# Twenty fields selected and twelve gathered in every unit, and each gather issued when the rows of the one in front of it have landed

## Chip, cores and metric

The kernel runs on one core of a Trainium2 chip. The metric is the device time in microseconds of one execution; of several executions the median counts.

## What is computed

A batch of 2048 samples has 32 categorical fields. Each field has its own table of rows of 64 floats (1000, 1250, 12500 or 125000 rows). For every sample the 32 rows are looked up, all pairs of them are multiplied (a Gram matrix of 32 by 32, of which the 496 entries above the diagonal count), 16 dense values are put behind, and a tower of three layers follows:

```python
e = jnp.stack([tbl_0[ids[:, 0]], ..., tbl_31[ids[:, 31]]], axis=1)
gram = jnp.einsum('bnd,bmd->bnm', e, e)
z = gram[:, rows, cols]                      # rows < cols
h = jnp.concatenate([z, dense_ctx], axis=1)
h = jnp.maximum(h @ W_top1 + b_top1, 0.0)    # 512 -> 512
h = jnp.maximum(h @ W_top2 + b_top2, 0.0)    # 512 -> 256
y = h @ W_top3                               # 256 -> 1
```

## The kernel before

The batch is cut into four units of 512 samples, and each unit into two rounds (halves of 256 samples). A field's rows reach the tensor `vecs` in one of two ways.

**Gathered fields.** GpSimd issues an indirect DMA (L296) that brings 128 rows of one field from its table in HBM into `rows`. One field, one round and one half of the round's samples make one gather; 16 fields make 64 gathers in a unit. TensorE turns them (`turn`, L513: a transposition into `gat_ps`, four fields together), and ScalarE copies them to `vecs` (L337). A turn waits until the semaphore `rows_in[r][x]` counts all its gathers, 16 counts for each. Between two gathers GpSimd writes zeros into a spare tile that nobody reads (L303): a fill of 1024 columns in unit 0 and of 512 in the others. A gather never waits for another. It waits only for the turn of the unit before that emptied its part of `rows` (L292).

**Selected fields.** Small tables (1000 or 1250 rows) are held on chip as three bf16 parts, `tabs`, packed so that a row number is a partition and a chunk: 8 chunks for 1000 rows, 10 for 1250. For each chunk VectorE compares the broadcast sample indices `ids_wide` with the chunk's row numbers and writes a one-hot matrix (L453). TensorE multiplies table parts and one-hots into `sel_ps` (`select`, L498): three matmuls for a chunk and field. Fields go in pairs; one-hots come in pieces (half of a field's chunks) through a ring of four. ScalarE copies the result to `vecs` (L329). The tables are loaded and split once, in unit 0, by `high` and `middle` on ScalarE (L317, L322) and two subtractions on VectorE (L436, L441). SP loads `ids_wide` for the next unit pair by pair, 256 KB each (L197), as soon as the one-hots of that pair are done.

In units 0 and 3 sixteen fields (eight pairs) are selected and sixteen gathered (four turns). In units 1 and 2 the last pair is gathered too: seven pairs, five turns, the last of them with two fields:

```python
SHIFTED = (1, 2)
ROWS_OF = GATHERED + SELECTED[-2:]
PAIRS = [ALL_PAIRS - (u in SHIFTED) for u in range(UNITS)]
TURNS = [ALL_TURNS - (u not in SHIFTED) for u in range(UNITS)]
```

**The rest of a unit.** When all 32 fields of a round are in `vecs`, TensorE forms the products (`gram`, L528: 512 small matmuls a round, in four calls). ScalarE and VectorE copy them to `work` (L346, L460), SP writes them to HBM (L206 to L209) and reads them back as diagonals (L224 to L228) for the tower (L542, L551, L560). The tower of a unit runs between the products of the next. All orders are written out by hand. On TensorE a unit is: the rest of its selection with the turns of round 0 among the last pairs; products of round 0 with the first layer of the unit before between them; the turns of round 1, with two selections of the next unit among them; products of round 1 with the second and third layer of the unit before between them. After unit 3 come the tower passes of its two rounds.

The names used below: `gather(u, r, x)` and `turn(u, r, x)` are for unit u, round r and group x of four fields.

## Time and profile before

| | us |
|---|---|
| median of 3 runs | 574.52 (572.3 to 587.05) |
| the profiled execution, its own time | 577.56 |
| its span, first to last instruction | 575.8 |
| GpSimd busy | 465.0 |
| TensorE busy | 403.8 |
| VectorE busy | 292.7 |
| ScalarE busy | 141.8 |

Busy time is the union of an engine's instructions. In the rows below an arrow names what a row waited for last, and a time in front of it the idle time that ended so. Positions are microseconds from the span's start. "PEclk" is the clock granted to TensorE as a share of 2.4 GHz. A DMA instruction's own row is the time for issuing it, not the time in which data move; these are seen in the DMA share, the mean busy share of the core's 16 DMA engines.

### The profile page before, as it was taken

What the parts mean: (1) busy time and instruction counts of PE and PEld (TensorE: products, weight loads), DVE (VectorE), ACT (ScalarE), POOL (GpSimd) and SP (SyncE); (2) the same over time, 40 slices, a digit from 0 to 9 for tenths busy, and PEclk for the clock granted to TensorE, in tenths of its full rate; (3) what the DMA queues carried; (4) which work ended last, traced back from release to release, by engine and by line L of the source; (5) the groups of instructions that cost most, each with busy time, mean ns of one, the idle gap of its engine ahead of it and who ended that gap; (6) DMA issues with size and microseconds to landing.
All of it is one profiled execution on the core that took longest, in us unless ns stands there. A gap on an engine that the chain in (4) does not pass through costs nothing.

```text
span 575.8 us, 13498 instructions
## 1 busy us (share of the span) xinstructions
PE 403.8 (70%) x5956; PEld 217.7 (38%) x5956; DVE 292.7 (51%) x513; ACT 141.8 (25%) x232; POOL 465.0 (81%) x552
## 2 busy tenths in 40 slices
PE   0556554756874678787975687868966788799877
PEld 0222222323543334334432344334432344445655
DVE  4999999999180299300810499100900599100000
ACT  5002233422200334310201434111110434212212
POOL 7999999999998899989998999889988999950000
PEclk9977778787695699888986799887996799989989
DMA  8414311110111475110111584101011651003340
GB/s 271 140 51 141 98 33 32 30 35 15 21 21 23 73 166 150 29 23 20 22 21 23 101 190 124 23 21 21 21 23 23 132 119 19 19 16 64 72 83 1
DMA packets 39060, 36.11 MB, mean 63 GB/s; under 512 B 14869, under 2 KB 27991, under 8 KB 38874
## 3 DMA queue, kind: packets, MB, share of 16 engines
q1 hardware_dynamic: 29866, 25.14, 18.0%
q0 software_dynamic: 8704, 8.93, 7.6%
q8 instruction: 47, 0.77, 0.5%
q10 hardware_dynamic: 432, 1.18, 0.5%
q14 instruction: 11, 0.09, 0.0%
HBM read 27.15 MB, written 8.07 MB: 61 GB/s over the span
## 4 chain that ended last, share of the span: by engine, by line
PE 42%; DVE 39%; issue 11%; ACT 4%; DMA 2%; SPq 2%; ACTq 0%; DVEq 0%
DVE onehot L453 35%; PE gram_ps L528 14%; PE tower_ps L542 11%; PE sel_ps L498 9%; PE tower_ps L551 5%; ACT vecs L329 2%; PE tower_ps L560 2%; DVE work L436 2%; DVE tabs L441 2%; PE gat_ps L513 2%; DMA work<-in_packed_dram 1%; ACT work L346 1%; SPq L207 1%; DMA products<-work 1%; SPq L209 1%
## 5 line engine op out<-in xcount | busy, mean ns | idle before, releaser
L453 DVE TENSOR_SCALAR onehot<-ids_wide,row_ids 128x512 bf16<-128x512 f16 x488 | 269.4, 627 | 113.2 <-PE sel_ps L498 113.2
L296 POOL DMA_INDIRECT rows<-in_tbl_dram,gat_ids x272 | 287.0, 1055 | 46.3 <-issue 44.3
L498 PE MATMUL sel_ps<-onehot,tabs 128*64 128x512 bf16 x1464 | 200.4, 433 | 98.1 <-DVE onehot L453 79.5
L303 POOL MEMSET spare<- 128x512 f32 (+1 forms) x272 | 177.9, 654 | 0.1
L498 PEld LDWEIGHTS sel_ps<-onehot,tabs 128*64 128x64 bf16 x1464 | 95.9, 123 | 196.8 <-issue 95.2
L528 PE MATMUL gram_ps<-vecs 64*32 64x32 f32 x4096 | 71.2, 214 | 61.4 <-issue 48.8
L329 ACT COPY vecs<-sel_ps 64x256 f32<-64x256 f32 x120 | 71.9, 599 | 123.1 <-PE sel_ps L498 70.2
L528 PEld LDWEIGHTS gram_ps<-vecs 64*32 64x32 f32 x4096 | 54.6, 115 | 93.7 <-issue 80.5
L542 PE MATMUL tower_ps<-work,w_sb 128*128 128x512 f32 (+1 forms) x160 | 73.8, 622 | 2.8 <-DMA work<-products 2.8
L460 DVE COPY work<-gram_ps 128x512 f32<-128x512 f32 x8 | 5.2, 687 | 127.9 <-PE gram_ps L528 127.9
L542 PEld LDWEIGHTS tower_ps<-work,w_sb 128*128 128x128 f32 x160 | 35.7, 230 | 31.4 <-issue 25.3
L352 ACT ACTIVATE h<-tower_ps,b_sb 128x512 f32<-128x512 f32 (+1 forms) x20 | 12.0, 602 | 81.2 <-PE tower_ps L542 81.2
L551 PE MATMUL tower_ps<-h,w_sb 128*128 128x512 f32 (+1 forms) x80 | 31.0, 537 | 1.1 <-ACT h L352 1.1
L337 ACT COPY vecs<-gat_ps 128x512 f32<-128x512 f32 (+1 forms) x36 | 19.5, 570 | 34.8 <-PE gat_ps L513 29.5
L346 ACT COPY work<-gram_ps 128x512 f32<-128x512 f32 x24 | 13.0, 588 | 59.3 <-PE gram_ps L528 59.3
L322 ACT CAST tabs<-work 128x1024 bf16<-128x1024 f32 (+1 forms) x8 | 8.6, 1072 | 70.0 <-DVE work L436 70.0
L513 PE MATMUL gat_ps<-ident,rows 128*128 128x128 f32 x136 | 21.7, 293 | 4.9 <-ACT vecs L337 4.9
L513 PEld LDWEIGHTS gat_ps<-ident,rows 128*128 128x128 f32 x136 | 15.1, 145 | 14.4 <-issue 8.6
L551 PEld LDWEIGHTS tower_ps<-h,w_sb 128*128 128x128 f32 x80 | 15.1, 197 | 12.5 <-issue 9.7
L359 ACT ACTIVATE h<-tower_ps,b_sb 128x512 f32<-128x512 f32 (+1 forms) x10 | 5.5, 598 | 36.3 <-PE tower_ps L551 36.3
L560 PE MATMUL tower_ps<-h,w_sb 128*1 128x512 f32 (+1 forms) x20 | 11.1, 689 | 1.9 <-ACT h L359 1.9
L436 DVE TENSOR_TENSOR work<-work,tabs 128x1024 f32<-128x1024 f32 (+1 forms) x8 | 10.0, 1248 | 4.2 <-ACT tabs L317 4.2
(13 smaller groups left out, 25.1 us busy)
## 6 DMA issues: line engine op xcount, KB each, us to landing
ids_wide<-ids_scratch SPq DMA_DIRECT2D x30, 256.0 KB
rows<-in_tbl_dram,gat_ids POOLq DMA_INDIRECT x272
products<-work SPq DMA_DIRECT2D x12, 248.0 KB
products<-work SPq DMA_DIRECT2D x24, 120.0 KB
work<-in_packed_dram SPq DMA_DIRECT2D x5, 512.0 KB, 4.4
work<-products SPq DMA_DIRECT2D x9, 256.0 KB
work<-in_packed_dram ACTq DMA_DIRECT2D x2, 512.0 KB, 6.1
w_sb<-in_w_dram SPq DMA_DIRECT2D x1, 1024.0 KB
```

The costliest lines, as they stand in the source:

```text
L296: nc.gpsimd.indirect_dma_start(out=rows[:, r, k, h, :], out_offset=None, in_=tables[ROWS_OF[k]], in_offset=bass.IndirectOffsetOnAxis(ap=ga ...
L303: nc.gpsimd.memset(spare[:, 0:SPACING[u]], 0.0).then_inc(spaced, 1)
L329: last = nc.scalar.copy(vecs[DIM * h:DIM * h + DIM, :, N_GAT + 2 * g + at], sel_ps[DIM * at:DIM * at + DIM, sel_no(u, g) % 2, HALF * h:HAL ...
L337: nc.scalar.copy(vecs[:, P * r:P * r + P, at], gat_ps[:, n % 2, 0:P * fields].rearrange("p (f j) -> p j f", f=fields))\
L436: nc.vector.tensor_tensor(piece, piece, tabs[:, c0:c0 + k, 0, :], ALU.subtract).then_inc(rest_ready, 1)
L453: last = nc.vector.tensor_scalar(onehot[:, n % RING, c - c0, :], ids_wide[:, k, :], row_ids[chunks[k]][:, c:c + 1], None, ALU.is_equal)
L498: last[at] = nc.tensor.matmul(sel_ps[DIM * at:DIM * at + DIM, n % 2, :], tabs[:, first_chunk[k] + c, part, :], onehot[:, piece_no(u, g, ha ...
L513: last = nc.tensor.transpose(gat_ps[:, n % 2, P * at:P * at + P], rows[:, r, k, :, :].rearrange("p h d -> p (h d)"), ident[:])
L528: last = nc.tensor.matmul(gram_ps[32 * s:32 * s + 32, h, i, :], v, v, start=True, stop=True, skip_group_check=True)
L542: last = nc.tensor.matmul(tower_ps[:, j % 2, 0:width], w1_sb[:, c, P * j:P * j + P], z[:, c, x0:x0 + width], start=(c == 0), stop=(c == Q ...
L551: last = nc.tensor.matmul(tower_ps[:, o, 0:width], w2_sb[:, j, P * o:P * o + P], h1[:, j, 0:width], start=(j == 0), stop=(j == J1 - 1), sk ...
L560: last = nc.tensor.matmul(tower_ps[0:1, 0, 0:width], w3_sb[:, o:o + 1], h2[:, o, 0:width], start=(o == 0), stop=(o == J2 - 1))
```

## The change

Four things change. All units have the same plan: ten pairs selected and three turns gathered, so twelve gathered fields. Six tables of 1250 rows are now among the selected ones: of the sixteen selected before, two had 1250 rows. The fills are gone. And each gather is followed by a wait for its own sixteen counts, so that GpSimd issues the next when all of its rows have landed. The last pairs of a unit (from the eighth on) are where the turns of round 0 stand.

```diff
-SELECTED = [7, 8, 9, 11, 12, 15, 17, 18, 20, 22, 24, 25, 27, 28, 30, 31]
+SELECTED = [7, 8, 9, 11, 12, 15, 17, 18, 20, 22, 24, 25, 27, 28, 16, 21, 23, 29, 30, 31]
 GATHERED = [f for f in range(FIELDS) if f not in SELECTED]
...
+GROUPS = [range(k, min(k + 4, N_GAT)) for k in range(0, N_GAT, 4)]
+N_PAIRS, N_TURNS = N_SEL // 2, len(GROUPS)
...
-SPACING = [1024, 512, 512, 512]
...
             def gather(u, r, x):
-                for v in [v for v in range(u) if x < TURNS[v]][-1:]:
-                    pool.wait_ge(gat_full, gat_no(v, r, x) + 1)
-                for k in range(N_ROWS)[turn_slots(x)]:
+                if u > 0:
+                    pool.wait_ge(gat_full, gat_no(u - 1, r, x) + 1)
+                for k in GROUPS[x]:
                     for h in range(2):
-                        at = ((u * ROUNDS + r) * 2 + h) * N_ROWS + k
+                        at = ((u * ROUNDS + r) * 2 + h) * N_GAT + k
                         nc.gpsimd.indirect_dma_start(
-                            out=rows[:, r, k, h, :], out_offset=None, in_=tables[ROWS_OF[k]],
+                            out=rows[:, r, k, h, :], out_offset=None, in_=tables[GATHERED[k]],
                             in_offset=bass.IndirectOffsetOnAxis(ap=gat_ids[:, at:at + 1], axis=0))\
                           .then_inc(rows_in[r][x], 16)
-                        spaced_no = next(count)
-                        if spaced_no > 0:
-                            pool.wait_ge(spaced, spaced_no)
-                        nc.gpsimd.memset(spare[:, 0:SPACING[u]], 0.0).then_inc(spaced, 1)
+
+                        so_far = 2 * len(GROUPS[x]) * u + 2 * (k - GROUPS[x].start) + h + 1
+                        pool.wait_ge(rows_in[r][x], 16 * so_far)
...
             for u in range(UNITS):
-                for g in range(2, PAIRS[u]):
+                for g in range(2, N_PAIRS):
                     select(u, g)
-                    if g >= 4:
-                        turn(u, 0, g - 4)
-                for x in range(PAIRS[u] - 4, TURNS[u]):
-                    turn(u, 0, x)
+                    if g >= N_PAIRS - N_TURNS:
+                        turn(u, 0, g - N_PAIRS + N_TURNS)
...
-                for x in range(3, TURNS[u]):
+                for x in range(3, N_TURNS):
                     turn(u, 1, x)
```

The other engines' loops run over `N_PAIRS` and `N_TURNS` in the same way: `load_wide` on SP has ten loads a unit, and the table loads and subtractions of unit 0 are ten.

GpSimd's instructions at the start of the gathers, before (`ident` is the unit matrix of the turns, `spare` the tile of the fills):

```order
L285 AFFINE_SELECT ident<-ident 128x128 [waits ident_zero]
L296 DMA rows<-in_tbl_dram,gat_ids 128x64 [waits gat_ids_in0]
L303 MEMSET spare 128x1024
L296 DMA rows<-in_tbl_dram,gat_ids 128x64
L303 MEMSET spare 128x1024 [waits spaced]
L296 DMA rows<-in_tbl_dram,gat_ids 128x64
L303 MEMSET spare 128x1024 [waits spaced]
```

And the same place now, up to the end of unit 0's gathers (an "x8" is eight such instructions one after the other):

```order
L252 AFFINE_SELECT ident<-ident 128x128 [waits ident_zero]
L261 DMA rows<-in_tbl_dram,gat_ids 128x64 [waits gat_ids_in0]
L261 DMA rows<-in_tbl_dram,gat_ids 128x64 [waits rows_in0_0] x8
L261 DMA rows<-in_tbl_dram,gat_ids 128x64 [waits rows_in0_1] x8
L261 DMA rows<-in_tbl_dram,gat_ids 128x64 [waits rows_in0_2] x8
L261 DMA rows<-in_tbl_dram,gat_ids 128x64 [waits rows_in1_0] x8
L261 DMA rows<-in_tbl_dram,gat_ids 128x64 [waits rows_in1_1] x8
L261 DMA rows<-in_tbl_dram,gat_ids 128x64 [waits rows_in1_2] x7
L261 DMA rows<-in_tbl_dram,gat_ids 128x64 [waits gat_full,gat_ids_in1,rows_in1_2]
```

Between the gathers stand no other instructions any more, and every gather but the first waits for the semaphore of the one in front of it.

TensorE's instructions from the products of unit 0, round 0, to the first layer in unit 1, before (`gram_ps` products, `gat_ps` turns, `sel_ps` selection, `tower_ps` tower):

```order
L528 MATMUL gram_ps<-vecs 32x32 x256
L513 MATMUL gat_ps<-ident,rows 128x128 x8
L498 MATMUL sel_ps<-onehot,tabs 64x512 x48
L513 MATMUL gat_ps<-ident,rows 128x128 x4
L498 MATMUL sel_ps<-onehot,tabs 64x512 x48
L513 MATMUL gat_ps<-ident,rows 128x128 x4
L528 MATMUL gram_ps<-vecs 32x32 x256
L498 MATMUL sel_ps<-onehot,tabs 64x512 x144
L513 MATMUL gat_ps<-ident,rows 128x128 x4
L498 MATMUL sel_ps<-onehot,tabs 64x512 x48
```

And now:

```order
L489 MATMUL gram_ps<-vecs 32x32 x256
L474 MATMUL gat_ps<-ident,rows 128x128 x8
L460 MATMUL sel_ps<-onehot,tabs 64x512 x48
L474 MATMUL gat_ps<-ident,rows 128x128 x4
L460 MATMUL sel_ps<-onehot,tabs 64x512 x48
L489 MATMUL gram_ps<-vecs 32x32 x256
L460 MATMUL sel_ps<-onehot,tabs 64x512 x300
L474 MATMUL gat_ps<-ident,rows 128x128 x4
L460 MATMUL sel_ps<-onehot,tabs 64x512 x60
```

The fourth turn of round 1 is gone; the third, turn (u, 1, 2), now is the last before the products. Behind them 300 matmuls of selection stand where 144 stood.

## Rows read from the trace of the kernel before

**Rows 1.** The page: its span, and section 1, busy time of each engine.
```profile
span 575.8 us, 13498 instructions
PE 403.8 (70%) x5956; PEld 217.7 (38%) x5956; DVE 292.7 (51%) x513; ACT 141.8 (25%) x232; POOL 465.0 (81%) x552
```
**Rows 2.** The chain that ended last: by line, then pieces (start us, us, what).
```profile
by line: DVE onehot L453 35.4%; PE gram_ps L528 13.5%; PE tower_ps L542 11.4%; issue 10.9%; PE sel_ps L498 9.0%; PE tower_ps L551 4.6%; ACT vecs L329 2.5%; PE tower_ps L560 1.7%; DVE work L436 1.6%; DVE tabs L441 1.6%; PE gat_ps L513 1.6%; 
...
87.02 6.33 DVE onehot L453 x8
...
206.36 6.90 DVE onehot L453 x16
...
243.84 3.63 PE tower_ps L542 x8
252.02 5.33 PE tower_ps L542 x8
...
272.93 2.75 PE sel_ps L498 x24
...
523.88 1.15 PE gat_ps L513 x8
...
557.63 10.00 PE tower_ps L542 x32
```
**Rows 3.** One line's instructions: gathers and one-hots (duration ns min/median/max, first and last start us).
```profile
L296 POOL DMA_INDIRECT rows<-in_tbl_dram,gat_ids x272: 950/1062/2204, 3.3 to 510.5; - x136
...
L453 DVE TENSOR_SCALAR onehot<-ids_wide,row_ids x488: 332/342/1759, 12.4 to 490.9; 128x512 bf16<-128x512 f16 x163
```
**Rows 4.** Groups by line and form (busy us, mean ns, idle before and releasers).
```profile
L296 POOL DMA_INDIRECT rows<-in_tbl_dram,gat_ids x272 | 287.0, 1055 | 46.3 <-issue 44.3 <-DMA gat_ids<-in_ids_gat_dram 1.8 <-PE gat_ps L513 0.2
L453 DVE TENSOR_SCALAR onehot<-ids_wide,row_ids 128x512 bf16<-128x512 f16 x488 | 269.4, 627 | 113.2 <-PE sel_ps L498 113.2
...
L303 POOL MEMSET spare<- 128x512 f32 x208 | 115.9, 557 | 0.1
...
L303 POOL MEMSET spare<- 128x1024 f32 x64 | 62.0, 969 | 0.0
...
L436 DVE TENSOR_TENSOR work<-work,tabs 128x1280 f32<-128x1280 f32 x1 | 1.5, 1472 | 0.0
```
**Rows 5.** Slices behind one gather (us; engines; then PEclk, DMA share, GB/s).
```profile
488.30:488.50 0.20, 0.20 (x6) 0.13 (x2) 0.20 (x1) 0.20 (x1) 0.20 (x1) 1.00 0.00 0
488.50:488.70 0.20, 0.20 (x6) 0.12 (x3) 0.20 (x2) 0.10 (x1) 0.04 (x1) 1.00 0.25 61
...
488.90:489.10 0.20, 0.20 (x6) 0.12 (x4) 0.20 (x2) 0.00 (x0) 0.20 (x1) 1.00 0.06 10
489.10:489.30 0.20, 0.20 (x6) 0.12 (x4) 0.20 (x2) 0.00 (x0) 0.20 (x1) 1.00 0.00 0
```
**Rows 6.** Timeline of GpSimd (start us, us; in brackets the idle time before).
```profile
3.31 1.19 POOL L296 DMA_INDIRECT rows<-in_tbl_dram,gat_ids  x1 [1.85 <-DMA gat_ids<-in_ids_gat_dram]
...
26.24 1.94 POOL L296 DMA_INDIRECT rows<-in_tbl_dram,gat_ids  x1 [0.17 <-issue]
...
486.90 1.07 POOL L296 DMA_INDIRECT rows<-in_tbl_dram,gat_ids  x1 [0.16 <-issue]
```
**Rows 7.** The page's section 6, DMA issues (KB each, median us to landing): the index load.
```profile
gat_ids<-in_ids_gat_dram SPq DMA_DIRECT2D x1, 36.0 KB, 2.3
```
**Rows 8.** Timeline of SP's queue: the index load, and the seven broadcasts for unit 2.
```profile
0.74 0.40 SPq L237 DMA_DIRECT2D gat_ids<-in_ids_gat_dram  x1
...
213.41 15.31 SPq L197 DMA_DIRECT2D ids_wide<-ids_scratch  x7
```
**Rows 9.** Slices before the last tower pass, columns as in rows 5.
```profile
556.60:556.80 0.20, 0.00 (x0) 0.00 (x0) 0.00 (x0) 0.00 (x0) 0.00 (x0) 0.50 0.18 51
556.80:557.00 0.20, 0.00 (x0) 0.00 (x0) 0.00 (x0) 0.00 (x0) 0.00 (x0) 0.50 0.02 5
```
**Rows 10.** Windows with busy transfer engines, the first and the last of five.
```profile
0.00:20.00 20.00, 1.08 (x6) 0.63 (x8) 11.48 (x14) 7.36 (x7) 16.41 (x23) 1.00 0.78 265
...
446.00:472.00 26.00, 19.93 (x150) 9.68 (x151) 19.38 (x43) 10.35 (x18) 23.60 (x30) 0.84 0.68 137
```

More of the change, by code:

```diff
@@ L44 @@
 MOVES = 3 * Q
-SPACING = [1024, 512, 512, 512]
-PAIRS = [ALL_PAIRS - (u in SHIFTED) for u in range(UNITS)]
-TURNS = [ALL_TURNS - (u not in SHIFTED) for u in range(UNITS)]
-PAIRS_TO = [sum(PAIRS[:u]) for u in range(UNITS + 1)]
-MOST_PAIRS = max(PAIRS)
-TURNS_TO = [ROUNDS * sum(TURNS[:u]) for u in range(UNITS + 1)]
 def sel_no(u, g):
-    return PAIRS_TO[u] + g
+    return N_PAIRS * u + g
 def gat_no(u, r, x):
-    return TURNS_TO[u] + TURNS[u] * r + x
-def units_with_pair(u, g):
-    return sum(g < PAIRS[v] for v in range(u))
-def units_with_turn(u, x):
-    return sum(x < TURNS[v] for v in range(u))
-def turn_slots(x):
-    return slice(4 * x, min(4 * x + 4, N_ROWS))
-def turn_columns(x):
-    return slice(4 * x, 4 * x + 4) if 4 * x < N_GAT else slice(FIELDS - 2, FIELDS)
+    return N_TURNS * (ROUNDS * u + r) + x
 def emptied_no(u, r, b):
@@ L86, in piece_no @@
 def piece_no(u, g, half, at):
-    return 4 * (PAIRS_TO[u] + g) + 2 * half + at
+    return 4 * (N_PAIRS * u + g) + 2 * half + at
 def pair_row(n, m):
@@ L99, in dlrm_tower_kernel @@
     half_most = max(b - a for h in halves for a, b in h)
-    pair_chunks = [(first_chunk[2 * g], chunks[2 * g] + chunks[2 * g + 1]) for g in range(ALL_PAIRS)]
+    pair_chunks = [(first_chunk[2 * g], chunks[2 * g] + chunks[2 * g + 1]) for g in range(N_PAIRS)]
     pair_most = max(k for _, k in pair_chunks)
-    assert all(chunks[2 * g] == chunks[2 * g + 1] for g in range(ALL_PAIRS))
+    assert all(chunks[2 * g] == chunks[2 * g + 1] for g in range(N_PAIRS))
     with ExitStack() as ctx:
@@ L121, in dlrm_tower_kernel @@
         onehot = sb("onehot", [P, RING, half_most, UNIT], BF16)
-        rows = sb("rows", [P, ROUNDS, N_ROWS, 2, DIM], F32)
+        rows = sb("rows", [P, ROUNDS, N_GAT, 2, DIM], F32)
         vecs = sb("vecs", [P, HALF, FIELDS], F32)
@@ L193, in load_wide @@
             def load_wide(u, w):
-                last = [v for v in range(u) if w < PAIRS[v]][-1:]
-                for v in last:
-                    sp.wait_ge(onehot_ready, piece_no(v, w, 1, 1) + 1)
+                if u > 0:
+                    sp.wait_ge(onehot_ready, piece_no(u - 1, w, 1, 1) + 1)
                 sp.dma_start(ids_wide[:, WIDE * w:WIDE * w + WIDE, :],
@@ L234, in store @@
                   .then_inc(y_out[v % 2], 16)
-            first = ROUNDS * 2 * N_ROWS
+            first = ROUNDS * 2 * N_GAT
             sp.dma_start(gat_ids[:, 0:first], ids_gat[:, 0:first]).then_inc(gat_ids_in[0], 16)
@@ L246, in _ @@
                 load_wide(0, w)
-            for g in range(STAGE_SLOTS, MOST_PAIRS):
+            for g in range(STAGE_SLOTS, N_PAIRS):
                 load_stage(g)
@@ L254, in _ @@
             for u in range(LAST):
-                for w in range(PAIRS[u + 1]):
+                for w in range(N_PAIRS):
                     load_wide(u + 1, w)
@@ L308, in _ @@
                 for r in range(ROUNDS):
-                    for x in range(TURNS[u]):
+                    for x in range(N_TURNS):
                         gather(u, r, x)
@@ L386, in _ @@
             for u in range(UNITS):
[L387 removed]
+                for g in range(2, N_PAIRS):
                     selected(u, g)
[L389 removed]
+                    if u == 0 and g + 4 < N_PAIRS:
                         high(g + 4)
                         middle(g + 4)
[L392 to L395 removed]
+                    if g >= N_PAIRS - N_TURNS:
+                        gathered(u, 0, g - N_PAIRS + N_TURNS)
                 if u == 0:
@@ L405, in _ @@
                 gram(u, 0, 1, (0, 1))
-                for x in range(TURNS[u]):
+                for x in range(N_TURNS):
                     gathered(u, 1, x)
@@ L445, in one_hots @@
                 if half == 0:
[L446 removed]
+                    dve.wait_ge(wide_in[g], 16 * (u + 1))
                 for at in range(2):
@@ L659 @@
     out = nc.dram_tensor("out_0_dram", (BATCH, 1), _mybir.dt.float32, kind="ExternalOutput").ap()
-    tables = {f: args[f"tbl_{f}"] for f in ROWS_OF}
+    tables = {f: args[f"tbl_{f}"] for f in GATHERED}
     chunks = [inputs[f"tbl_{f}"].shape[0] // KROWS for f in SELECTED]
```

48 lines of the change are left out of this document (18 added, 30 removed).

## The prediction

> **What bounds the kernel now.** I began with the shares of the span [rows 1]. GpSimd is busy 465.0 of 575.8 us, more than TensorE (403.8) or VectorE (292.7). The next view to read is the chain of work that ended last [rows 2]: 35% of it is the one-hot instructions of VectorE, the rest mostly TensorE, and GpSimd is not in it. So GpSimd is fullest and yet holds nobody up. The source view of the gathers says why [rows 3]: 272 gathers, the last issued at 510.5 us; before them GpSimd waited 44.3 us for "issue" (0.16 us each), 1.8 us for its index load and 0.2 us for TensorE. It runs without a break from 3.3 us, gather and fill in turn, at a pace that the program chose: 1055 ns for a gather, 557 or 969 ns for a fill [rows 4]. The chain takes up the last transposes at 523.88 [rows 2], some 11 us after those rows came in. The pace of the gathers is hidden, but by about 2% of the span only. That is the number to hold on to.
>
> VectorE is slowed by the same fills. Its one-hots last 332 ns at least and 342 in the median, but 627 in the mean and 1759 at most [rows 3, 4]. In unit 0, with the long fills, eight follow each other in 6.33 us (0.79 us each); later, with short fills, sixteen take 6.9 us (0.43 each) [rows 2]. The Trainium skill ("SBUF — State Buffer", on the shared port pair) says that a VectorE instruction in a two-port mode and a GpSimd instruction exclude each other for their whole length. The trace agrees in size: a 1759 ns one-hot is 1417 ns over the median, one long fill of 969 and some 450 of the gather in front of it. So the fills' removal helps VectorE whatever else happens, and the gathers' share of its delays stays.
>
> **The change, part by part.**
>
> Fills. 272 of them go, 177.9 us of GpSimd [rows 4].
>
> Fields. One-hots rise from 488 to 4 × (14×8 + 6×10) = 688, selecting matmuls from 1464 to 2064, gathers fall from 272 to 4 × 2 × 12 × 2 = 192. Without fills I take 0.34 us for a one-hot, so a unit costs VectorE 172 × 0.34 = 58 us. TensorE needs about 2.8 us for the 24 matmuls of half a pair [rows 2], so a unit's 14 halves of 24 and 6 halves of 30 take 14×2.8 + 6×3.4 = 60 us. Unit 0, where the first plan spent 132 × 0.79 = 104 us on one-hots, saves about 37 us net of six more table subtractions of 1.47 us [rows 4]. Units 1 and 2 have three pairs more and two turns fewer: about +12 us each. Unit 3 has 8 pairs after its first two where it had 6, but each at TensorE's pace: about nothing. So TensorE's and VectorE's side, if nothing else held it, would shrink by 37 − 24 = 13 us, and by up to 24 us more where the issue gaps of TensorE in the pair products get fewer. This is the gain that the change could have.
>
> The new wait. Every gather now waits until the rows of the one before it have landed. Queued behind that wait on GpSimd is nothing but the other gathers; the order shows it. TensorE waits for them: turn (u,1,2) needs all 48 gathers of its unit, and behind it in TensorE's stream stand the second half's pair products and the next unit's selection. So GpSimd's time becomes one sum, 192 times the cycle of a gather.
>
> The cycle has three pieces. (1) From the start of a gather to the end of its data. The gather that starts at 486.90 [rows 6] has its traffic in the slices from 488.5 to 489.1, with silence before and after [rows 5]: 2.0 to 2.2 us. (2) From the data's end to the semaphore, and (3) from the semaphore to the next start. The trace never shows GpSimd waiting for gathered rows, so these are bounded by neighbours. At the kernel's start the index load, issued at 0.74, lands 2.3 us later, at 3.04, and GpSimd's first gather starts at 3.31: 0.27 us for (3) [rows 6 to 8]. The last wait of TensorE for a transfer gives (2) and (3) together: the share of the DMA engines is down to 0.02 at 556.8 to 557.0, and the matmul starts at 557.63: 0.65 us or a little more [rows 2, 9]. Lower end: 2.1 + 0.45 = 2.55 us. Upper end: 2.2 + 0.75 = 2.95 us. I take 2.7. Against it stands the 1.7 us of gather, fill and issue on which the old kernel ran (1.06 + 0.56 + 0.16, [rows 4]). Even with no fill the new cycle is a microsecond longer; 192 × 2.7 = 518 us, where 272 gathers took 507.
>
> On this the Trainium skill ("DMA: Bandwidth & Descriptors", on the anatomy of a DMA issued by GpSimd) speaks for the change: about 2.0 us plus bytes over 436 GB/s from issue to completion. By its figures, as an estimate, a gather of 32 KB would take 2.08 us and 192 of them 399 us, and they would be hidden with ease. The trace does not agree: the data alone end after 2.0 to 2.2 us, and the semaphore and the restart come on top.
>
> Busy transfer engines. In five stretches the share of the DMA engines is 0.68 to 0.78: 0 to 20, 48 to 62, 194 to 228, 320 to 350 and 446 to 472, in all 124 us (the first and the last of the five stand in [rows 10]). There a gather's packets stand among those of the broadcasts and the products. Ten more broadcasts of 256 KB (40 for 30) at 15.31/7 = 2.2 us each [rows 8] add 22 us: 146 us. Before, such a delay cost nothing, since GpSimd didn't look; now each is on the path. A gather in such a stretch may be held by nothing or by a whole broadcast (2.2 us), and two to three things are queued there, so I take 1.5 us: 146/4.2 = 35 gathers × 1.5 = 52 us. Bounds: 20 and 66 us. In unit 0 a table subtraction can hold a gather (1.94 us instead of 1.07 [rows 6]): 20 subtractions × 0.35 = 7 us.
>
> The tail. From the last transposes at 523.88 to the span's end are 52 us [rows 1, 2]. It stays, since every step hangs on the last rows: the second layer, the last products, their way through memory, the last tower passes. After a wait of some 20 us TensorE would begin it at the lower of its two levels, as at 556.6 to 557.0 after a short pause [rows 9] (granted clock 0.50 is 1.2 GHz, 1.00 is 2.4). Eight tower matmuls take 5.3 us where the clock is low for 3.6 at the full one [rows 2]; two such groups come first, so I add 3 us.
>
> **The sum.** 3.3 (start) + 518 + 52 + 7 + 52 + 3 = 635 us of span. The profiled execution was 577.6 for a span of 575.8, so 637; the median of the runs shown is 3 us under the profiled time, so 634 us. GpSimd ends its last gather near 581 us instead of 512, and drags the rest along. TensorE's gain of 13 us or more disappears in its wait for turn (u,1,2).
>
> **Rivals.**
> (a) The gathers remain hidden, and the faster VectorE shows. That needs a cycle of at most 2.45 us and little delay in busy stretches: 192 × 2.45 = 470, so the last rows land at 475 to 490. The end is then TensorE's: 574.5 − 13 = 561 down to 537, say 548 us. For it: 465 us of GpSimd work shrink to 203 us of gathers, and VectorE is 35% of the chain. Against it: the pieces of the cycle measure more. It decides from a cycle of 2.5 us down. Chance 0.06.
> (b) The new wait just cancels the gain. Cycle 2.55 us, busy stretches cost 20 us: 3.3 + 490 + 20 + 52 = 565, time 564 to 586. For it: one gather in flight at a time may slip through the queues better than two. Chance 0.10.
> (c) Worse than forecast. Cycle 2.95 us, 66 us in busy stretches, 14 us from the subtractions and a tail of 55: 705 us; in part, above 668. For it: the 0.65 us between data and matmul at the end. Against it: that one moved more data to HBM and back. Chance 0.08.
> Forecast 0.76.
>
> **Range.** Low end: cycle 2.6 (499) + 3.3 + 30 + 52 + 1.8 = 586. High end: 2.8 (538) + 3.3 + 66 + 7 + 55 = 669. A measurement of this kernel can tell about 2% from no change (563 to 586). Slower by more: (c), the forecast: 0.84. Within: (b) 0.10. Faster by more: (a) 0.06.
>
> **What would show it.** GpSimd's gathers start 2.6 to 2.8 us apart in quiet stretches, and about 4 in those with a DMA share near 0.7; the last one starts near 578 us of the span. The releaser of GpSimd's waits is the DMA of rows; TensorE's transposes show long waits of 10 us and more once a unit; the one-hots' mean is near their old median of 342 ns, and VectorE and TensorE are busy less than 60% of the span. The granted clock falls in each wait. Wrong would be the sum if starts lie under 2.5 us apart, if the last transposes don't wait, or if the time from them to the end isn't 50 to 56 us.

## The result, and the profile after

The changed kernel takes 675.27 us (673.14 to 677.21, four executions) beside 573.41 us (571.43 to 587.05) of the kernel before: a ratio of 1.178, 95% interval 1.174 to 1.183. Some executions of a kernel run longer at a lower granted clock; medians and ranges here are of all executions, ratios leave those out, and "like with like" below does too. The forecast was 634 us with a range of 586 to 669. The direction and the mechanism came true, and the time lies 6 us above the range.

The page of the changed kernel, its span, busy times, granted clock and DMA share, the chain that ended last, and two of its groups (columns as in [rows 1, 4]):

```profile
span 671.3 us, 14540 instructions
PE 420.5 (63%) x6516; PEld 234.6 (35%) x6516; DVE 222.4 (33%) x717; ACT 166.6 (25%) x264; POOL 204.0 (30%) x200
...
PEclk9999975557759987957698996957688999755899
DMA  7453100000037410000007710000007300320040
...
DMA 77%; issue 13%; PE 5%; POOL 3%; SPq 1%; DVE 0%; ACT 0%; POOLq 0%
...
L261 POOL DMA_INDIRECT rows<-in_tbl_dram,gat_ids x192 | 203.1, 1058 | 411.2 <-DMA rows<-in_tbl_dram,gat_ids 405.2
L415 DVE TENSOR_SCALAR onehot<-ids_wide,row_ids 128x512 bf16<-128x512 f16 x688 | 193.7, 354 | 279.4 <-PE sel_ps L460 278.0
...
L474 PE MATMUL gat_ps<-ident,rows 128*128 128x128 f32 x96 | 20.9, 356 | 187.4 <-DMA rows<-in_tbl_dram,gat_ids 187.4
```

GpSimd has fallen from the fullest engine (81% in [rows 1]) to one of the emptiest (30%), and is now the bound. Busy shares hide this; the chain shows it. Before, it consisted of one-hots and matmuls [rows 2]; now 77% of it is DMA, nearly all of it the landing of gathered rows. The idle time before the gathers, 46.3 us in [rows 4], is 411.2, of which 405.2 ended with rows that landed. TensorE's turns wait 187.4 us for the same rows. Each long stretch of 5 to 7 in PEclk is such a wait.

The waits of the changed kernel: engine and line, what for, us in all, times, longest:

```profile
POOL rows L261 <- DMA rows<-in_tbl_dram,gat_ids: 405.2, 190, 5.4
DVE onehot L415 <- PE sel_ps L460: 278.0, 55, 65.7
...
PE gat_ps L474 <- DMA rows<-in_tbl_dram,gat_ids: 187.4, 14, 21.3
```

VectorE's 278 us are the longest of all in this list after the gathers, and mean nothing: its one-hots are early, and wait for TensorE to free the ring.

The source view of the gathers and of the one-hots (as [rows 3]), and how long a gather's rows took to land:

```profile
L261 POOL DMA_INDIRECT rows<-in_tbl_dram,gat_ids x192: 943/946/4463, 3.4 to 614.8; - x192
...
DMA to landing us min/median/max: 2.3/2.5/8.3
```

A quiet place, GpSimd's timeline (as [rows 6]) and the slices behind the gather at 126.91 (as [rows 5]):

```profile
124.17 0.94 POOL L261 DMA_INDIRECT rows<-in_tbl_dram,gat_ids  x1 [1.72 <-DMA rows<-in_tbl_dram,gat_ids]
126.91 0.95 POOL L261 DMA_INDIRECT rows<-in_tbl_dram,gat_ids  x1 [1.80 <-DMA rows<-in_tbl_dram,gat_ids]
129.60 0.95 POOL L261 DMA_INDIRECT rows<-in_tbl_dram,gat_ids  x1 [1.74 <-DMA rows<-in_tbl_dram,gat_ids]
```
```profile
128.30:128.50 0.20, 0.00 (x0) 0.00 (x0) 0.00 (x0) 0.00 (x0) 0.00 (x0) 0.50 0.00 0
128.50:128.70 0.20, 0.00 (x0) 0.00 (x0) 0.00 (x0) 0.00 (x0) 0.00 (x0) 0.50 0.74 124
128.70:128.90 0.20, 0.00 (x0) 0.00 (x0) 0.00 (x0) 0.00 (x0) 0.00 (x0) 0.50 0.27 41
128.90:129.10 0.20, 0.00 (x0) 0.00 (x0) 0.00 (x0) 0.00 (x0) 0.00 (x0) 0.50 0.02 0
129.10:129.30 0.20, 0.00 (x0) 0.00 (x0) 0.00 (x0) 0.00 (x0) 0.00 (x0) 0.50 0.00 0
```

Starts are 2.74 and 2.69 us apart. Nothing moves for the first 1.6 us; the data are through in some 0.4 us; then 0.6 to 0.7 us pass until the next start. The transfer itself is the small part of a cycle.

The same in windows of 24 gathers each, the eight halves of the four units (columns: length; busy time and count of TensorE, its weight loads, VectorE, ScalarE, GpSimd; granted clock; DMA share; GB/s):

```profile
3.40:104.50 101.10, 61.27 (x525) 31.41 (x526) 76.46 (x209) 47.11 (x63) 38.82 (x25) 0.93 0.39 131
104.50:172.80 68.30, 18.39 (x573) 11.95 (x574) 4.65 (x16) 3.91 (x7) 22.67 (x25) 0.55 0.07 12
172.80:258.70 85.90, 64.02 (x993) 36.61 (x993) 44.80 (x158) 27.09 (x45) 25.43 (x25) 0.84 0.33 77
258.70:326.10 67.40, 31.32 (x605) 16.57 (x605) 4.40 (x16) 6.56 (x11) 22.65 (x25) 0.73 0.07 13
326.10:409.50 83.40, 71.69 (x1013) 39.13 (x1014) 44.92 (x158) 28.90 (x48) 24.48 (x24) 0.93 0.35 79
409.50:475.70 66.20, 32.90 (x605) 17.13 (x606) 4.64 (x16) 6.56 (x11) 22.76 (x24) 0.71 0.07 13
475.70:550.10 74.40, 69.75 (x978) 37.97 (x980) 41.00 (x142) 26.54 (x44) 23.56 (x25) 0.92 0.28 53
550.10:617.50 67.40, 26.65 (x593) 14.58 (x590) 0.00 (x0) 8.94 (x15) 22.64 (x24) 0.72 0.19 36
```

This table is the whole result. At 2.7 us a cycle, 24 gathers take 64.8 us. The second half of every unit comes close (66.2 to 68.3: together 10 us more than four times 64.8). The first halves, in which one-hots, broadcasts and products run, take 101.1, 85.9, 83.4 and 74.4: 86 us more than 2.7 a cycle. In the second halves TensorE is busy for 18 to 33 us of 67, and its granted clock is 0.55 to 0.73.

### The profile page after: what moved, and what is told of

The parts are those of the page before. It is cut to its first block, busy times and chain, and to the rows that moved or that the text cites. A ratio compares the mean times of both kernels' runs of the same rounds, so it can differ in the third digit from the quotient of the medians.

```text
span 671.3 us, 14540 instructions
## 1 busy us (share of the span) xinstructions
PE 420.5 (63%) x6516; PEld 234.6 (35%) x6516; DVE 222.4 (33%) x717; ACT 166.6 (25%) x264; POOL 204.0 (30%) x200
## 2 busy tenths in 40 slices
DMA packets 38232, 37.48 MB, mean 56 GB/s; under 512 B 13781, under 2 KB 26903, under 8 KB 38042
## 4 chain that ended last, share of the span: by engine, by line
DMA 77%; issue 13%; PE 5%; POOL 3%; SPq 1%; DVE 0%; ACT 0%; POOLq 0%
DMA rows<-in_tbl_dram,gat_ids 76%; POOL rows L261 3%; PE tower_ps L512 2%; PE tower_ps L503 1%; PE gram_ps L489 1%; PE tower_ps L521 1%; SPq L176 1%; DMA products<-work 0%; DMA gat_ids<-in_ids_gat_dram 0%; DMA work<-products 0%; SPq L174 0%; SPq L173 0%; DVE work L422 0%; SPq L191 0%; PE gat_ps L474 0%
## 5 line engine op out<-in xcount | busy, mean ns | idle before, releaser
L261 POOL DMA_INDIRECT rows<-in_tbl_dram,gat_ids x192 | 203.1, 1058 | 411.2 <-DMA rows<-in_tbl_dram,gat_ids 405.2
L415 DVE TENSOR_SCALAR onehot<-ids_wide,row_ids 128x512 bf16<-128x512 f16 x688 | 193.7, 354 | 279.4 <-PE sel_ps L460 278.0
L460 PE MATMUL sel_ps<-onehot,tabs 128*64 128x512 bf16 x2064 | 247.7, 401 | 34.2 <-ACT vecs L293 17.9
L460 PEld LDWEIGHTS sel_ps<-onehot,tabs 128*64 128x64 bf16 x2064 | 128.7, 116 | 148.3 <-issue 48.4
L474 PE MATMUL gat_ps<-ident,rows 128*128 128x128 f32 x96 | 20.9, 356 | 187.4 <-DMA rows<-in_tbl_dram,gat_ids 187.4
L293 ACT COPY vecs<-sel_ps 64x256 f32<-64x256 f32 x160 | 96.7, 605 | 105.4 <-PE sel_ps L460 93.4
L301 ACT COPY vecs<-gat_ps 128x512 f32<-128x512 f32 x24 | 14.1, 588 | 206.6 <-PE gat_ps L474 206.4
L489 PE MATMUL gram_ps<-vecs 64*32 64x32 f32 x4096 | 50.7, 210 | 22.0 <-issue 14.1
L489 PEld LDWEIGHTS gram_ps<-vecs 64*32 64x32 f32 x4096 | 43.5, 112 | 45.1 <-issue 37.3
L286 ACT CAST tabs<-work 128x1024 bf16<-128x1024 f32 (+1 forms) x10 | 11.1, 1109 | 26.3 <-DVE work L398 26.3
L403 DVE TENSOR_TENSOR tabs<-work,tabs 128x1024 bf16<-128x1024 f32 (+1 forms) x10 | 13.0, 1295 | 1.1 <-ACT tabs L286 1.1
L281 ACT CAST tabs<-work 128x1024 bf16<-128x1024 f32 (+1 forms) x10 | 11.1, 1108 | 3.5 <-DMA work<-in_packed_dram 3.4
```

The source lines that it names most:

```text
L261: nc.gpsimd.indirect_dma_start(out=rows[:, r, k, h, :], out_offset=None, in_=tables[GATHERED[k]], in_offset=bass.IndirectOffsetOnAxis(ap=g ...
L293: last = nc.scalar.copy(vecs[DIM * h:DIM * h + DIM, :, N_GAT + 2 * g + at], sel_ps[DIM * at:DIM * at + DIM, sel_no(u, g) % 2, HALF * h:HAL ...
L301: nc.scalar.copy(vecs[:, P * r:P * r + P, at:at + fields], gat_ps[:, n % 2, 0:P * fields].rearrange("p (f j) -> p j f", f=fields))\
L403: nc.vector.tensor_tensor(tabs[:, c0:c0 + k, 2, :], stage[g % STAGE_SLOTS][:, 0:k, :], tabs[:, c0:c0 + k, 1, :], ALU.subtract).then_inc(ta ...
L415: last = nc.vector.tensor_scalar(onehot[:, n % RING, c - c0, :], ids_wide[:, k, :], row_ids[chunks[k]][:, c:c + 1], None, ALU.is_equal)
L460: last[at] = nc.tensor.matmul(sel_ps[DIM * at:DIM * at + DIM, n % 2, :], tabs[:, first_chunk[k] + c, part, :], onehot[:, piece_no(u, g, ha ...
```

## The experiments

The runs were made on four chips, here A to D, which give the kernel before 557.6 (A), 567 (B), 557.1 (C) and 557.9 us (D). Each ratio is to the kernel before on the same chip. It matters below. On which chip the first measurement ran isn't on record; the kernel before took 573.41 us there, more than on any of the four.

**Which part of the change costs the time.** First the changed kernel without its wait, nothing else (chip A):

```diff
-                        so_far = 2 * len(GROUPS[x]) * u + 2 * (k - GROUPS[x].start) + h + 1
-                        pool.wait_ge(rows_in[r][x], 16 * so_far)
```

> The changed kernel without the wait behind each gather (still no fills). Theory (the serial cycle of 192 gathers is the whole slowdown): GpSimd issues gathers every 1.1 to 1.2 us, is held only by the turns of the unit before, the transposes no longer wait 187 us, and the time is that of TensorE's side, 530 to 565 us. Rival (the field split, 2064 selecting matmuls for 1464, is what costs): 620 us or more, with TensorE waiting for one-hots or ScalarE instead.

Measured: 461.84 us, ratio 0.829 (0.824 to 0.834). The page's line of the gathers, and the products:

```profile
L261 POOL DMA_INDIRECT rows<-in_tbl_dram,gat_ids x192 | 186.3, 970 | 152.0 <-PE gat_ps L471 93.4 <-issue 56.7 <-DMA gat_ids<-in_ids_gat_dram 1.9
...
L486 PE MATMUL gram_ps<-vecs 64*32 64x32 f32 x4096 | 53.0, 209 | 18.8 <-issue 8.8 <-ACT work L307 4.9 <-ACT vecs L298 2.7
```

The gathers wait for TensorE again, which empties their tensor, and not for their rows. The two lines of code cost some 210 us: the changed kernel takes 672 to 677 us on every chip that ran it. The version is faster by far more than I had expected of it; why it is, and that it isn't on every chip, comes below.

Then the new split of fields with the fills as they were, in place of the wait (chip A):

```diff
-                        so_far = 2 * len(GROUPS[x]) * u + 2 * (k - GROUPS[x].start) + h + 1
-                        pool.wait_ge(rows_in[r][x], 16 * so_far)
+                        spaced_no = next(count)
+                        if spaced_no > 0:
+                            pool.wait_ge(spaced, spaced_no)
+                        nc.gpsimd.memset(spare[:, 0:SPACING[u]], 0.0).then_inc(spaced, 1)
```

> The new field split with the old fills (1024 columns in unit 0, 512 after) instead of the wait. Theory: gathers go out every 1.75 to 2.2 us, 192 of them end by 400 us and hold nobody; one-hots are back at 0.43 us in the later units and 0.79 in unit 0, so about 172 x 0.79 = 136 us for unit 0's selection and 172 x 0.43 = 74 for each other unit: 590 to 630 us, slower than without fills by 40 us or more. Rival (fills cost VectorE nothing on the path): same as the run without them, within 1%.

Measured: 529.69 us, ratio 0.951 (0.947 to 0.956). So I was wrong on the sign: twenty selected fields are worth 28 us even with the fills, although the one-hots last 515 ns in the mean (in the profile of an execution of 541.43 us).

And the other half alone, the old split with the wait in place of the fills (chip A, one execution):

```diff
-                        spaced_no = next(count)
-                        if spaced_no > 0:
-                            pool.wait_ge(spaced, spaced_no)
-                        nc.gpsimd.memset(spare[:, 0:SPACING[u]], 0.0).then_inc(spaced, 1)
+                        landed[r, x] = landed.get((r, x), 0) + 1
+                        pool.wait_ge(rows_in[r][x], 16 * landed[r, x])
```

> The kernel before with the new wait in place of the fills, field split as before (272 gathers). Theory: GpSimd's chain is 3.3 + 272 x 2.70 = 738 us and 90 to 100 us of delays in stretches with busy transfer engines, plus 54 of tail: about 885 us. Rival (the split costs, not the wait): below 675 us.

Measured: 881.98 us, as expected. Its waits:

```profile
POOL rows L296 <- DMA rows<-in_tbl_dram,gat_ids: 536.0, 268, 6.4
...
PE gat_ps L511 <- DMA rows<-in_tbl_dram,gat_ids: 442.2, 31, 22.8
```

The rule "so many gathers by one cycle, plus delays, plus the tail" carries over to 272 gathers. The two parts of the change are nothing alike: the split gains, the wait loses, and the fewer gathers of the new split only soften the wait.

**Is it the wait as such, or one gather at a time?** A semaphore for each half h, and each gather waits for the one before the last, so that two are in flight (chip A):

```diff
-        rows_in = [[sem(f"rows_in{r}_{x}") for x in range(N_TURNS)] for r in range(ROUNDS)]
+        rows_in = [[[sem(f"rows_in{r}_{x}_{h}") for h in range(2)] for x in range(N_TURNS)] for r in range(ROUNDS)]
...
+                        if landing[h]:
+                            pool.wait_ge(*landing[h])
...
-                          .then_inc(rows_in[r][x], 16)
+                          .then_inc(rows_in[r][x][h], 16)
...
+                        landing[h] = (rows_in[r][x][h], 16 * (len(GROUPS[x]) * u + k - GROUPS[x].start + 1))
```

> The changed kernel with two gathers in flight: each half h has a semaphore of its own and a gather waits for the rows of the one before the last. Theory: two gathers per cycle of 2.7 to 2.9 us, 192 in about 270 us plus delays, so GpSimd is never last outside unit 0 and the time is that of the run without waits, within 2%. Rival (GpSimd needs the whole landing time for itself, or the port is the limit): cycle of a gather stays above 2 us, time above 600 us.

Measured: 471.31 us, ratio 0.841 (0.831 to 0.850), 2% over the kernel without the wait. GpSimd still waits 141.7 us for rows, and it costs 9 us. What hurt was that a whole landing stood between any two gathers.

**What lengthens the cycle in the first halves.** The changed kernel once more on chip B:

> The changed kernel itself, as the yardstick for the other runs of this call: 660 to 680 us, GpSimd's gathers 2.7 us apart in quiet stretches.

Measured: 677.43 us, ratio 1.196 (1.185 to 1.206).

Theory one: a gather is held as long as VectorE's one-hots follow each other without a gap. In units 1 to 3 each one-hot gets a second one in front, which nobody reads (chip B):

```diff
+                        if u > 0:
+                            no = next(extras)
+                            if no >= 4:
+                                dve.wait_ge(extra_done, no - 3)
+                            nc.vector.tensor_scalar(extra[:, no % 4, :], ids_wide[:, k, :],
+                                                    row_ids[chunks[k]][:, c:c + 1], None, ALU.is_equal)\
+                              .then_inc(extra_done, 1)
```

> The changed kernel with a second, unused one-hot ahead of each one-hot in units 1 to 3, so that VectorE has fewer gaps there. Theory (a gather that starts while VectorE's one-hots follow without a gap is kept from finishing until the next gap, as in unit 0): the gathers' mean in the selection stretches of the later units rises from 0.95 to 1.06 us to 1.5 us or more, with single ones of 3 us and over, and the time by 20 to 60 us over the changed kernel. Rival (unit 0's long gathers come from the table loads and subtractions there): gathers stay at 0.94 to 1.1 us in the later units, and the time within 1% of the changed kernel.

Measured: 847.02 us (825.68 to 849.09): 170 us over the unchanged kernel, and like with like still 148, where I expected 20 to 60. GpSimd's gathers are busy for 392.4 us, 2044 ns each in the mean, beside 195.8 us and 1020 ns in the unchanged kernel on the same chip, so the gathers that last longer account for the loss and more. The gathers by source, and a piece of GpSimd's timeline:

```profile
L263 POOL DMA_INDIRECT rows<-in_tbl_dram,gat_ids x192: 942/942/54732, 3.3 to 790.5; - x192
```
```profile
635.11 5.57 POOL L263 DMA_INDIRECT rows<-in_tbl_dram,gat_ids  x1 [2.71 <-DMA rows<-in_tbl_dram,gat_ids]
643.32 54.73 POOL L263 DMA_INDIRECT rows<-in_tbl_dram,gat_ids  x1 [2.64 <-DMA rows<-in_tbl_dram,gat_ids]
699.74 0.94 POOL L263 DMA_INDIRECT rows<-in_tbl_dram,gat_ids  x1 [1.69 <-DMA rows<-in_tbl_dram,gat_ids]
```

One gather lasts 54.73 us where the median is 0.94. Over that stretch VectorE shows:

```profile
643.40:698.00 54.60, 32.38 (x268) 16.54 (x268) 53.84 (x206) 14.46 (x25) 54.60 (x1) 0.94 0.09 20
```

It is busy 53.84 of 54.60 us with 206 instructions, and the DMA share is 0.09, so it isn't busy transfer engines that hold the gather. It fits the mechanism for which the prediction cited the Trainium skill ("SBUF — State Buffer", "Who interferes with whom", on the shared port pair): VectorE in a two-port mode and GpSimd exclude each other. The trace doesn't show the ports or the mode of a one-hot; it shows that the two engines don't take turns here: VectorE, back to back, kept the gather out for 54 us. In the changed kernel gathers are held for a shorter time. GpSimd's gathers in unit 0, while one-hots and table subtractions follow each other:

```profile
24.12 4.46 POOL L261 DMA_INDIRECT rows<-in_tbl_dram,gat_ids  x1 [1.84 <-DMA rows<-in_tbl_dram,gat_ids]
30.31 3.34 POOL L261 DMA_INDIRECT rows<-in_tbl_dram,gat_ids  x1 [1.73 <-DMA rows<-in_tbl_dram,gat_ids]
...
40.49 3.17 POOL L261 DMA_INDIRECT rows<-in_tbl_dram,gat_ids  x1 [3.45 <-DMA rows<-in_tbl_dram,gat_ids]
```
```profile
23.05 2.19 DVE L415 TENSOR_SCALAR onehot<-ids_wide,row_ids 128x512 bf16<-128x512 f16 x8
25.15 1.22 DVE L398 TENSOR_TENSOR work<-work,tabs 128x1024 f32<-128x1024 f32 x1
26.28 2.19 DVE L415 TENSOR_SCALAR onehot<-ids_wide,row_ids 128x512 bf16<-128x512 f16 x8
```

All gathers together are 21.7 us over 192 × 0.945 (busy 203.1), 16 of it in the first half of unit 0 (38.82 − 22.7 in the window table). There each of the ten gathers that last over 1.3 us overlaps a table subtraction as well as one-hots, so that what each of the two holds isn't separated; in units 1 to 3, where one-hots are alone, it is some 6 us, with single gathers of 2.83 and 1.93 us. And gathers were held before the change, too: 272 of them were busy for 287.0 us [rows 4], 30 us over 272 × 0.945, but nobody waited for them.

Theory two: the broadcasts hold the gathers. In units 1 to 3 they bring 32 of the 512 samples' indices, and what the one-hots of those units select is left wrong (chip B):

```diff
-                sp.dma_start(ids_wide[:, WIDE * w:WIDE * w + WIDE, :],
-                             ids_scratch[u, WIDE * w:WIDE * w + WIDE, :].partition_broadcast(P))\
+                n = UNIT if u == 0 else UNIT // 16
+                sp.dma_start(ids_wide[:, WIDE * w:WIDE * w + WIDE, 0:n],
+                             ids_scratch[u, WIDE * w:WIDE * w + WIDE, 0:n].partition_broadcast(P))\
```

> The changed kernel with the index broadcasts of units 1 to 3 cut to 32 of 512 samples (the other samples keep the indices of unit 0, so their selected rows are those of other samples). Theory (half of the delays in busy stretches is the broadcasts'): GpSimd's chain gets shorter by 30 to 45 us, time 630 to 645. Rival (the products on their way through memory, or something else, delay the gathers): less than 12 us shorter, 660 or more.

Measured: 669.96 us, ratio 1.179 (1.170 to 1.188), 7 us under the unchanged one on the same chip. Its first halves of units 1 to 3:

```profile
170.60:252.60 82.00, 64.78 (x993) 37.57 (x994) 45.27 (x158) 27.10 (x45) 24.20 (x25) 0.85 0.28 51
320.90:403.50 82.60, 70.55 (x1013) 38.96 (x1014) 45.44 (x158) 28.97 (x48) 26.18 (x24) 0.93 0.28 50
469.20:546.30 77.10, 70.04 (x978) 38.00 (x980) 41.24 (x142) 26.52 (x44) 23.50 (x25) 0.91 0.27 51
```

They take 241.7 us where those of the unchanged kernel on chip B take 247.8 (85.1, 84.7, 78.0). So the bytes of the broadcasts cost 6 to 7 us. What the broadcasts as such cost isn't settled: all thirty still run, with 16 KB in place of 256, land after 4.8 us in the median where 5.7 was usual, and the run has more packets than before (42072 for 38232).

Theory three, what is left: the transfers of products. Each of the twelve writes of units 0 to 2 is made twice, the second time into a tensor that nobody reads (chip C):

```diff
                 for s in range(Q):
-                    rows_out(u, s, slice(0, P), slice(P * s, P * s + P))
+                    rows_out(u, s, slice(0, P), slice(P * s, P * s + P), products)
+                    rows_out(u, s, slice(0, P), slice(P * s, P * s + P), copies)
```

> The changed kernel; in units 0 to 2 each of the twelve writes of products is made twice, the second time into a tensor that nobody reads. Theory: a gather waits its turn among the transfers of products, about 1.6 us each, in some 20 us per unit, of which the writes are more than half. Twice the writes are some 10 us more of such a stretch per unit, with periods of 4 to 5 us where 2.7 stood: 8 to 14 us a unit, so 700 to 717 us. Rival: the excess comes from instruction loads and TensorE's or VectorE's work in that phase, not from the transfers: 675 to 685 us.

Measured: 690.32 us (682.20 to 697.45), beside 671.87 (664.71 to 687.43) of the changed kernel, moved by 1056 bytes, on the same chip. Like with like it is 684.5 beside 667.1 us (two executions and three): 17 us, where I expected 28 to 45. The same three windows:

```profile
178.00:263.80 85.80, 63.77 (x993) 37.17 (x994) 44.98 (x158) 27.06 (x45) 24.70 (x25) 0.86 0.45 100
...
331.00:416.00 85.00, 69.83 (x1013) 38.63 (x1014) 45.83 (x158) 28.95 (x48) 23.40 (x25) 0.94 0.46 101
...
481.00:563.30 82.30, 73.08 (x1013) 39.58 (x1014) 40.92 (x142) 28.87 (x48) 24.80 (x24) 0.93 0.38 73
```

The DMA share rises from 0.34, 0.34 and 0.26 in the profile of the moved kernel to 0.45, 0.46 and 0.38. The windows alone don't show the cost: they take 253.1 us, and those of the moved kernel, profiled in its execution of 687.43 us, 252.6 (86.9, 85.7, 80.0). The packet records show it. In units 1 to 3, 12 gathers of the moved kernel land late while SP issues writes of products or just behind them, by 21 us in all; with the writes doubled it is 23 gathers and 33 us. (On the other two chips the unchanged kernel has 14 gathers and 17 us, and 13 and 18.) So transfers of products do hold gathers, and twice the writes hold about twice as many, each for no longer: a gather started at 205.17, amid the doubled writes, has its successor 3.33 us later, and one at 200.56, amid the single ones of the changed kernel, 3.33 us later too. That is 12 to 16 us more for the three units, where I expected 24 to 42.

**Why 462 us, and not everywhere.** On chip B three kernels with bare gathers, no fill and no wait. First the old split:

```diff
-                        spaced_no = next(count)
-                        if spaced_no > 0:
-                            pool.wait_ge(spaced, spaced_no)
-                        nc.gpsimd.memset(spare[:, 0:SPACING[u]], 0.0).then_inc(spaced, 1)
```

> The kernel before with neither fills nor waits, 272 gathers one behind the other. Theory (the fills alone held the old kernel, and the new split is worth little by itself): gathers 1.25 us apart, 470 to 490 us. Rival (the gain over the old kernel that was seen without waits comes from the new split): above 520 us.

Measured: 666.20 us, ratio 1.171 (1.163 to 1.179): 100 us slower than with the fills, where the new split without its wait had been 17% faster on chip A. Two of its lines:

```profile
L494 PE MATMUL sel_ps<-onehot,tabs 128*64 128x512 bf16 x1464 | 215.8, 419 | 139.9 <-issue 92.3 <-DVE onehot L449 35.2 <-ACT vecs L325 10.3
...
L524 PE MATMUL gram_ps<-vecs 64*32 64x32 f32 x4096 | 64.3, 215 | 94.8 <-issue 82.4 <-ACT vecs L333 6.8 <-ACT work L342 4.7
```

TensorE stands idle with "issue", that is, for no reason that the profile knows. I looked for it in the split, by sixteen selected fields in all units (old kernel, bare) and by eighteen (new kernel, bare):

```diff
-SHIFTED = (1, 2)
+SHIFTED = ()
```

> Sixteen fields selected and sixteen gathered in all units, no fills, no waits (256 gathers). Theory S with the number of gathers as the cause: between 560 and 660 us, with stalls beside the gathers in proportion to 256 against 272. If only the fifth turn did it: below 520 us. Theory P says nothing about it.

```diff
-SELECTED = [7, 8, 9, 11, 12, 15, 17, 18, 20, 22, 24, 25, 27, 28, 16, 21, 23, 29, 30, 31]
+SELECTED = [7, 8, 9, 11, 12, 15, 17, 18, 20, 22, 24, 25, 27, 28, 16, 21, 30, 31]
```

> Eighteen fields selected and fourteen gathered in all units (fourth turn with two fields), no fills, no waits: 224 gathers. Without stalls in TensorE's issue it has 20 one-hots and 60 selecting matmuls a unit less than the version with twenty and twelve, some 7 us a unit less for TensorE and one turn more: 440 to 455 us, faster than 462. With stalls as in the old split: 520 us or more.

Measured: 645.15 and 621.36 us, ratios 1.136 (1.128 to 1.144) and 1.096 (1.089 to 1.104). And in the placement of the tensors in memory, by an unused tensor of 264 words in front of all others, once with the old split and once with the new one:

```diff
+        pad = sb("pad", [P, 264], F32)
         ident = sb("ident", [P, P], F32)
```

> The old split with neither fills nor waits, and one unused tensor of 264 words a partition allocated first, so that all tensors on chip lie 1056 bytes further up; nothing else differs. Theory P (TensorE's issue stalls of 0.7 us beside gathers depend on where the tensors lie): the time moves by more than 5% from 666 us. Theory S (they belong to the old split itself, more gathers and other streams): 650 to 680 us, the stalls as before.

> The new split with neither fills nor waits, and the same unused tensor in front. Theory P: the stalls come in, and the time rises from 462 us by more than 5%. Theory S: 455 to 472 us, no stalls.

Measured: 665.36 us, the same as unmoved on this chip (666.20), and 622.41 us, ratio 1.096 (1.090 to 1.103). The second looked like a proof: the kernel of 461.84 us, moved by 1056 bytes, takes 160 us more. It was none, since the two had run on different chips. Smaller moves on chip C, by 256 and by 8 words in place of 264, didn't bring the stalls back:

> The kernel without the wait, all tensors 1024 bytes higher (before: 1056 bytes made it 622 us where it took 462). If the 32 bytes beyond a multiple of 1024 (or of 64) decide, this one is back at 460 to 475 us; if the move by a kilobyte decides, it is near 620 us.

> The kernel without the wait, all tensors 32 bytes higher. If the alignment to 64 bytes decides, near 620 us; if only moves of about a kilobyte matter, 460 to 475 us. Should both this and the move by 1024 bytes stay near 462, neither part alone explains the 622.

Measured: 464.24 and 465.81 us, ratios 0.836 both. So the two kernels of the false proof ran side by side on chip D:

> The kernel without the wait once more, beside the one moved by 1056 bytes on the same chip. Until now the two were timed on different chips. If placement makes the difference: 460 to 470 us. If the chip makes it, this one is slow here when the moved one is, near 620 us, or both are near 465.

> The kernel without the wait and all tensors 1056 bytes higher, once more, beside the unmoved one on the same chip. If placement makes the difference: 615 to 625 us beside 460 to 470 for the unmoved one. If the chip or the run makes it, the two are within 2% of each other.

Measured: 465.15 us and 466.52 us. Placement does nothing, neither on chip D nor, with the old split, on chip B. The same kernel takes 622 us on chip B and 467 us on chip D. TensorE's timeline on chip B, then on chip D:

```profile
43.30 0.58 PE L458 MATMUL sel_ps<-onehot,tabs 128*64 128x512 bf16 x1 [2.90 <-issue]
45.41 0.59 PE L458 MATMUL sel_ps<-onehot,tabs 128*64 128x512 bf16 x1 [1.52 <-issue]
48.20 0.58 PE L458 MATMUL sel_ps<-onehot,tabs 128*64 128x512 bf16 x1 [2.21 <-issue]
```
```profile
38.61 5.56 PE L458 MATMUL sel_ps<-onehot,tabs 128*64 128x512 bf16 x48 [1.93 <-ACT vecs L291]
46.09 5.57 PE L458 MATMUL sel_ps<-onehot,tabs 128*64 128x512 bf16 x48 [1.92 <-ACT vecs L291]
```

On B there is one matmul in 2.1 to 2.8 us; on D 48 of the same instructions take 5.56 us. In both GpSimd issues a gather every 1.25 us. With the wait nothing of this shows in the time: on chip B, where bare gathers bring the stalls, the changed kernel takes 677.43 us. Moved by the same 1056 bytes it also ran on chip C, where bare gathers bring none:

> The changed kernel with an unused tensor of 264 words in front, so that all its tensors lie 1056 bytes higher. The same move made the kernel without the wait 160 us slower. Theory: with the wait, gathers are the bound and TensorE has some 38% of the span to spare, so stalls of TensorE are hidden: 665 to 690 us. Rival: the stalls also fall between the last rows of a round and the products, and into the tail, or stretch the gathers themselves: over 700 us.

Measured: 671.87 us (664.71 to 687.43).

## Why the prediction was wrong

Its mechanism was right, step by step.

- *The wait makes one sum of GpSimd's time.* Shown by the chain and, in isolation, by the runs without the wait (461.84), with two in flight (471.31) and with the wait alone (881.98).
- *A cycle of 2.7 us,* from three neighbouring rows and never seen before. Measured 2.69 and 2.74 in the rows above, 66.2 us for 24 in the quietest half (2.76). The data end after 2.0 to 2.2 us as read from [rows 5], and 0.6 us for semaphore and restart were in the bracket of 0.45 to 0.75. The formula of the Trainium skill ("DMA: Bandwidth & Descriptors", anatomy of a GpSimd-issued DMA), about 2.0 us plus bytes over 436 GB/s, gives 2.08 us as an estimate by its figures. The trace doesn't agree: the measured landing is 2.3 us at least and 2.5 in the median.
- *The tail of 52 + 3.* The last gather starts at 614.83 and lands 2.46 later; to the end of the span are 54 us.
- *TensorE's turns wait.* 187.4 us in 14 waits of up to 21.3, the last of them before the tail.
- *One-hots near 342 ns.* 354 in the mean. TensorE's 63% is above the 60% I named, VectorE's 33% below.

**The step that failed** is the delay of gathers beyond the quiet cycle: "35 gathers × 1.5 = 52 us" in busy stretches and "20 subtractions × 0.35 = 7 us", 59 us in all. Measured: from the first gather's start at 3.4 to the last landing at 617.3 are 613.9 us, less 518 makes 96 us. The quiet cycle was 2.69 us, which takes 2 us off; the rest, 98 us, is by the window table and a count over the packet records:

- gathers held on GpSimd: 22 us for 7. I had charged the table subtractions, one gather at a time by 0.35 us. That VectorE's one-hots hold gathers for as long as they follow each other is shown by the run in which they were doubled. How much of the 16 us in unit 0 is theirs and how much the subtractions', no run separates. The amount differs between profiles of the changed kernel: by the same count 14 us on chip B and 28 on chip C.
- gathers that land late beside transfers of the other queues: some 63 us (38 gathers by 1.7) for 52. Number and size were near. By what SP was issuing, 20 us of it belong to the first half of unit 0 with its loads, 19 to the writes of products, and 24 to the rest, mostly the reads and broadcasts behind the writes. The writes' part is borne out by the run that doubled them, and 6 to 7 us are the bytes of the broadcasts; the rest is read from the trace, not taken apart by a run.
- gathers that land late beside loads of instructions, 16 KB each: some 13 us (17 gathers by 0.8), for which I had nothing. Of the 110 gathers behind which no other queue moved anything, none was late by more than 0.11 us. Such loads stand in the packet records of before as well, where they delayed nobody. No run took them away, so this part is read from the trace, not shown.

So three terms were too small, by 15, 11 and 13 us, the third of them put at nothing. With 96 in place of 59 the forecast's sum is 3.3 + 518 + 96 + 52 + 3 = 672 us of span, for 671.3 measured.

The range failed in the same place. Its high end took 66 us for the busy stretches and 7 for the subtractions, 73 together, and a cycle of 2.8 us gave 19 more: 92 us, where the delays alone came to 96. I bounded a sum of 192 waits by bounds on one source of delay, and left the sources I hadn't counted at nothing.

Two readings were off without an effect on the forecast. The changed kernel has 20 table subtractions and the one before 16, so four more and not six. And gather, fill and issue add up to 1.78 us, not 1.7; 272 gathers in 507 us are 1.86 each.

**A second size was wrong, without an effect on the forecast:** rival (a), the gathers hidden, was priced at 548 us. On chips A, C and D the kernel without the wait takes 462 to 467. The gain had two parts. That TensorE's and VectorE's side shrinks by 13 to 37 us was right: with the fills kept it is 28 us. The other 68 us come from the fills that go, with which VectorE's one-hots fall from 515 to 367 ns in the mean and TensorE's mean granted clock rises from 0.91 to 0.96 (0.85 before the change). On chip B the same kernel, moved by 1056 bytes, is slower than before by 10%. For the chip of the first measurement, on which the kernel before takes 573 us, neither is known: no bare kernel is known to have run there.

## What to carry to other kernels

A wait for a DMA's landing behind every issue turns a hidden latency into a sum. Here 2.7 us stood where 1.25 was possible, and two in flight already brought back nearly all of it; ask for the depth of the queue before asking for the price of the wait. Once such a sum is the bound, every delay counts that was free before: price all sources that touch the waited-for transfer, on the issuing engine (VectorE's gap-free stretches), in the queues, and perhaps in instruction loads, and widen the range for those that you can't count. And compare kernels only on the same chip: a difference of 160 us that looked like placement was the chip.

## What the runs showed of the hardware that I had not expected

- A gather on GpSimd can be kept waiting for as long as VectorE issues one-hots (f16 in, bf16 out) without a gap: 54.73 us in one case.
- A quiet gather of 32 KB, 128 rows of 256 bytes, is 1.6 to 1.7 us of silence, 0.4 to 0.5 us of data and 0.6 us until a waiting GpSimd starts the next one.
- Chips differ by more than the kernel before tells. On one chip TensorE stalls beside gathers that follow each other every 1.25 us, in idle times of 1.5 to 2.9 us between single matmuls, and the kernel takes 622 us; on three others it doesn't, and takes 462 to 467. The kernel before differs by 1.8% between them. Gathers spaced by fills or by the wait don't bring the stalls out: the kernel before takes 567 us and the changed one 677 us on that chip. What differs in the chip, or in its state at that time, stays open, as does whether two gathers in flight would stall there; that kernel ran on chip A alone.
